# A second norm whose square, small operations and scaling stand one step later in the last chunk

## The chip, the cores and the metric

The kernel runs on the 8 cores of one Trainium2 chip, one batch element on each core, without any exchange between them. The metric is the device time of one execution in microseconds, taken for the slowest core.

## The reference

```python
x_dbl = einsum('bld,kd->blk', x, x_proj_w)           # 128 + 16 + 16 columns
delta = softplus(einsum('blr,dr->bld', x_dbl[..., :128], dt_proj_w) + dt_proj_b)
state = exp(delta * A) * state + delta * Bm * x      # a scan over 2048 tokens, 16 states
y     = einsum('bdn,bn->bd', state, c) + x * D_param
r     = layernorm(x + y)
e     = einsum('bln,nk->blk', r, weight) * scale     # 2048 x 2048
e     = e * tanh(|e|) / (|e| + eps), then clipped to a norm of 0.99
out   = layernorm(r + e)
```

x is (8, 2048, 2048), float32.

## The kernel before

The tokens of a core are taken in four chunks of 512 (chunk 0 to 3, LAST = 3). In a chunk there are 16 tiles of 128 channels, and for each of them 8 pairs of states: 128 steps to a chunk, 512 in all, numbered k. Step k of the scan is one instruction of VectorE (L1563). It takes decays from ScalarE (L1198 and L1200, two instructions for each step, issued two steps ahead) and inputs from TensorE (L881, into the two halves of pa). Five of eight steps then have their product with C made by GpSimd (g, L636) and summed by TensorE with an identity matrix (L841, L843); the other three are transposed by DMA from SyncE's queue (hT, L445) and multiplied on TensorE (L860). TensorE does this sum seven steps behind (LAG = 7), in the same in-order queue as the inputs of the next steps. After each tile of channels ScalarE evicts the sum as r_b (L1236), and the first sum of the next tile (L841) waits for that eviction by the semaphore r_ev.

Every engine's program is a loop over k, and all work beside the scans is put at written-out steps in it. While chunk c is scanned, the feed-forward part of chunk c - 1 runs beside it: transposes of r, a matrix product, a norm over the channels, and then for four blocks tb of 128 tokens the second layernorm. The blocks start at the steps S_R2 = (89, 98, 107, 116) of the chunk, and r2_at(k, after) says which block, if any, stands `after` steps behind its start at step k. A block goes as follows.

- after 0, ScalarE: scales eT by the factor ff and sums it (L1363).
- after 1, GpSimd: adds eT and rT into the buffer r2_b (L740, gpsimd_r2), and four small operations. In chunk 3 the add of blocks 1 to 3 first waits until the store of the block before has landed (out_p, L737).
- after 3, ScalarE: the square of r2_b with its sum (L1394, scalar_r2sq), which waits for the add.
- after 4, ScalarE: three small operations that make rq and nmr (L1374 to L1380).
- after 5: the norm itself, in place in r2_b. In chunks 1 and 2 ScalarE does it and SyncE stores it at after 6; in chunk 3 (blocks of chunk 2) GpSimd does it (L754, gpsimd_norm), waits for its own result and issues the store of 1 MB (L759).

There is one r2_b, so a block's add, square, norm and store exclude those of the next.

At the end of the last chunk SyncE transposes r (L490, the steps RT_LAST and then the rest); the first of these transposes waits until the add of block 3 is done (r2, L489), since that add reads the buffer rT that it overwrites. SyncE's queue is in order, and the transposes of h stand between those of r. After the last product and the last y matmul TensorE runs the rest of the feed-forward product for chunk 3 (tensor_rest, L1054), and then the norms of chunk 3 follow in series.

Of the kernel before, what the change touches and what calls it, by code (L numbers as in the profile page):

```python
# [21 lines left out]
STEPS = NDT * NP  # L22
# [30 lines left out]
LAST = NCH - 1  # L53
# [52 lines left out]
def n_row(c, name, tb=None):  # L106

    base = c * (len(ROWS) + NTB * len(PER_TB))
    if tb is None:
        return base + ROWS.index(name) + 1  # L110
    return base + len(ROWS) + tb * len(PER_TB) + PER_TB.index(name) + 1
# [11 lines left out]
def n_a2(c, tb):  # L123
    return c * NTB + tb + 1


def r2_at(k, after):

    for c in range(LAST):
        for tb in range(NTB):  # L130
            if (c + 1) * STEPS + S_R2[tb] + after == k:
                return c, tb
    return None
# [66 lines left out]
class K:  # L200
# [135 lines left out]
    def t(s, name):  # L336

        names = ("mean", "srr", "see", "r2sum", "r2sq", "lnq", "rq", "nmr",
# [4 lines left out]
        return s.tok[:, names.index(name), :]  # L343
# [183 lines left out]
    def gpsimd_program(s, e):  # L527
        S = s.sem
        for q in range(4):
            e.dma_start(out=s.c_xpw[:, q * 4:q * 4 + 4, :],  # L530
                        in_=s.xpw_d[:, q * 4:q * 4 + 4, :]
                        ).then_inc(S["xpw%d" % q], 16)
            s.gpsimd_x(e, 0, q)
        e.dma_start(out=s.c_dtw[:], in_=s.dtw_d).then_inc(S["dtw_in"], 16)
        s.tile_u(e, 0)
        for p in range(NH, 5):
            s.diag_b(e, 0, p, S["diag"])
        s.tile_u(e, 1)
        for p in range(5, NP):
            s.diag_b(e, 0, p, S["diag"])  # L540
        s.diag_c(e, 0, 0)
        for k in range(NK):
            c, st = divmod(k, STEPS)
            j, p = divmod(k, NP)
            if k > 0 and (k - 1) % NP in GP:
                s.gpsimd_cmul(e, k - 1)
            if k in (2, 4):
                s.diag_c(e, 0, k // 2)
            if p == 4 and j + 2 < NJ:
                s.tile_u(e, j + 2)  # L550
            if p == 6 and NDT <= j + 2 < NJ:
                s.gpsimd_carry(e, j + 2)
            for g in range(NKT):
                if k == S_CAST + SUM_GAP * g:
                    if g >= 2:
                        e.wait_ge(S["wc%d" % (g % 2)], g // 2 * 16)
                    e.dma_start(out=s.wbf_d[g], in_=s.wsw_d[g]
                                ).then_inc(S["wc%d" % (g % 2)], 16)
            for q in range(4):
                if c + 1 < NCH and st == (S_XQ if c > 0 else S_XQ0)[q]:  # L560
                    s.gpsimd_x(e, c + 1, q)
            if c + 1 < NCH and st >= STEPS - NP:
                s.diag_b(e, c + 1, st - (STEPS - NP), S["diag"])
            if 1 <= c < NCH and st + 1 in TP:
                s.diag_c(e, c, TP.index(st + 1))
            if 1 <= c <= LAST:
                s.token_values(e, c - 1, st)
            hit = r2_at(k, 1)
            if hit:
                s.gpsimd_r2(e, *hit)  # L570
            hit = r2_at(k, 5)
            if hit and hit[0] == LAST - 1:
                s.gpsimd_norm(e, hit[1])
        s.gpsimd_cmul(e, NK - 1)
        for kt in range(N_EARLY, NKT):
            s.load_w_rest(e, kt)
        for kt in range(NKT):
            s.gpsimd_prod(e, kt)
# [772 lines left out]
    def scalar_r2(s, e, k):  # L1351
        S = s.sem
        act = e.activation
        t = s.t

        def after_row(c, name, tb=None):
            e.wait_ge(S["row"], n_row(c, name, tb))

        hit = r2_at(k, 0)
        if hit:  # L1360
            c, tb = hit
            after_row(c, "ff")
            act(s.eT[:, tb, :], s.eT[:, tb, :], AF.Copy,  # L1363
                scale=t("ff")[:, tb:tb + 1],
                accum_out=t("r2sum")[:, tb:tb + 1]).then_inc(S["fe"], 1)
        if r2_at(k, 3):
            s.scalar_r2sq(e, *r2_at(k, 3))
        if r2_at(k, 4):
            c, tb = r2_at(k, 4)
            col = slice(tb, tb + 1)  # L1370
            n = n_a2(c, tb)
            after_row(c, "bq", tb)
            e.wait_ge(S["sq"], n)
            act(t("lnq")[:, col], t("r2sq")[:, col], AF.Ln, scale=RD,  # L1374
                bias=t("bq")[:, col]).then_inc(S["lnq"], 1)
            e.wait_ge(S["lnq"], n)
            act(t("rq")[:, col], t("lnq")[:, col], AF.Exp, scale=-0.5
                ).then_inc(S["rq"], 1)
            e.wait_ge(S["rq"], n)
            act(t("nmr")[:, col], t("nm")[:, col], AF.Copy,  # L1380
                scale=t("rq")[:, col]).then_inc(S["nmr"], 1)
        hit = r2_at(k, 5)
        if hit and hit[0] < LAST - 1:
            c, tb = hit
            col = slice(tb, tb + 1)
            e.wait_ge(S["nmr"], n_a2(c, tb))
            act(s.r2_b[:], s.r2_b[:], AF.Identity,
                scale=t("rq")[:, col], bias=t("nmr")[:, col]
                ).then_inc(S["o_ev"], 1)
# [220 lines left out]
```

## Time and profile before

| what | us |
|---|---|
| median of 3 runs | 1232.92 (1232.04 to 1249.09) |
| the profiled execution | 1232.44 |
| its span on the slowest core, core 4 | 1230.9 |
| VectorE busy in the span | 1152.6 |
| ScalarE busy | 996.6 |
| GpSimd busy | 961.0 |
| TensorE matmuls busy | 924.1 |

The profile is one execution. Times in its rows are microseconds from the start of the core's span. An idle time in brackets is that of the engine just before the instruction, with what the profile takes for its releaser; where an instruction waits for several semaphores, that is the one that came last by the profile. In rows that merge several instructions the duration covers all of them.

### The profile page before, as it was taken

What the parts mean: (1) busy time and instruction counts of PE and PEld (TensorE: products, weight loads), DVE (VectorE), ACT (ScalarE), POOL (GpSimd) and SP (SyncE); (2) the same over time, 40 slices, a digit from 0 to 9 for tenths busy, and PEclk for the clock granted to TensorE, in tenths of its full rate; (3) what the DMA queues carried; (4) which work ended last, traced back from release to release, by engine and by line L of the source; (5) the groups of instructions that cost most, each with busy time, mean ns of one, the idle gap of its engine ahead of it and who ended that gap; (6) DMA issues with size and microseconds to landing.
All of it is one profiled execution on the core that took longest, in us unless ns stands there. A gap on an engine that the chain in (4) does not pass through costs nothing.

```text
span 1230.9 us, 28298 instructions; the slowest of 8 cores (1222.2 to 1230.9 us)
## 1 busy us (share of the span) xinstructions
PE 924.1 (75%) x8772; PEld 587.1 (48%) x8932; DVE 1152.6 (94%) x597; ACT 996.6 (81%) x1730; POOL 961.0 (78%) x657
## 2 busy tenths in 40 slices
PE   4556666776689996666689997676569998688991
PEld 1344444544455554444455554444345555455551
DVE  1998999999999999999999999999999999998955
ACT  1676777777788899999877899999968798998854
POOL 2996766777997676898997677789998676789981
PEclk9597888888899999988789999888899999998995
DMA  8499979775659996245649997443468986357776
GB/s 114 102 134 142 137 117 148 118 123 99 138 91 186 159 181 102 54 99 106 141 84 168 183 161 121 66 96 108 122 111 141 179 151 132 55 141 166 183 162 168
DMA packets 337216, 159.67 MB, mean 130 GB/s; under 512 B 311280, under 2 KB 321104, under 8 KB 335280
## 3 DMA queue, kind: packets, MB, share of 16 engines
q1 hardware_dynamic: 326400, 134.66, 58.4%
q0 software_dynamic: 10672, 23.20, 11.5%
q8 instruction: 76, 1.25, 0.4%
q14 instruction: 68, 0.56, 0.2%
HBM read 83.29 MB, written 25.23 MB: 88 GB/s over the span
## 4 chain that ended last, share of the span: by engine, by line
ACT 26%; DVE 25%; issue 22%; PE 10%; POOL 9%; DMA 4%; SPq 1%; ACTq 1%; DVEq 0%; POOLq 0%; another core or an unknown queue 0%
DVE h L1563 25%; ACT dae_x L1200 12%; ACT dae_x L1198 7%; POOL g L636 4%; PE pa L881 2%; PE pb L961 2%; POOL r_b L740 2%; DMA c_dtw<-dtw 2%; DMA w_sl<-wbf 2%; ACT delta L1181 1%; PE pb L860 1%; ACT r_b L1236 1%; POOL diagC L659 1%; ACT delta L1187 1%; PE pa L1054 1%
## 5 line engine op out<-in xcount | busy, mean ns | idle before, releaser
L1563 DVE TENSOR_TENSOR_SCAN h<-dae_x,pa 128x1024 bf16<-128x1024 f32 x512 | 1118.2, 2262 | 23.8 <-PE pa L881 15.6
L636 POOL TENSOR_TENSOR g<-h,C_rep 128x1024 bf16<-128x1024 bf16 x320 | 678.4, 2127 | 194.0 <-DVE h L1563 185.0
L881 PE MATMUL pa<-diagB,uT 128*128 128x128 bf16 x4096 | 364.7, 232 | 224.0 <-DVE h L1563 212.4
L1198 ACT ACTIVATE dae_x<-delta,c_A 128x512 f32<-128x512 bf16 x512 | 367.0, 717 | 158.6 <-DVE h L1563 157.2
L881 PEld LDWEIGHTS pa<-diagB,uT 128*128 128x128 bf16 x4096 | 271.7, 102 | 397.0 <-issue 379.3
L1200 ACT ACTIVATE dae_x<-delta,c_A 128x511 f32<-128x511 bf16 x512 | 361.6, 706 | 0.0
L961 PE MATMUL pb<-r_b,w_sl 128*128 128x512 bf16 x747 | 192.5, 379 | 1.8 <-DMA w_sl<-wbf 0.7
L843 PE MATMUL pb<-g,eye_b 128*128 128x512 bf16 x319 | 132.7, 416 | 11.6 <-issue 3.7
L860 PE MATMUL pb<-diagC,hT 128*128 128x128 bf16 x1536 | 131.2, 235 | 0.5 <-DMA hT<-h 0.5
L860 PEld LDWEIGHTS pb<-diagC,hT 128*128 128x128 bf16 x1536 | 109.6, 107 | 21.4 <-issue 9.8
L961 PEld LDWEIGHTS pb<-r_b,w_sl 128*128 128x128 bf16 x768 | 71.9, 98 | 74.2 <-issue 2.2
L841 PE MATMUL pb<-g,eye_b 128*128 128x512 bf16 x213 | 89.0, 418 | 15.6 <-ACT r_b L1236 8.1
L612 POOL TENSOR_TENSOR u_b<-delta,x_b 128x512 bf16<-128x512 bf16 x64 | 75.0, 1171 | 21.8 <-ACT delta L1187 21.8
L889 PE MATMUL pa<-carry,eye_b 128*128 128x1 bf16 x768 | 75.0, 167 | 0.0
L889 PEld LDWEIGHTS pa<-carry,eye_b 128*128 128x128 bf16 x768 | 61.9, 102 | 0.2
L647 POOL TENSOR_TENSOR diagB<-eye_b,bcT 128x1024 bf16<-128x1024 bf16 x30 | 57.7, 1934 | 0.0
L740 POOL TENSOR_TENSOR r_b<-eT,rT 128x2048 f32<-128x2048 bf16 x12 | 48.8, 4069 | 9.6 <-ACT eT L1363 9.6
L992 PE MATMUL pb<-r_b,w_sl 128*128 128x512 bf16 x172 | 46.0, 387 | 1.9 <-DMA w_sl<-wbf 1.5
L841 PEld LDWEIGHTS pb<-g,eye_b 128*128 128x128 bf16 x320 | 33.9, 106 | 21.6 <-issue 21.5
L1181 ACT ACTIVATE delta<-pb,c_dtb 128x512 bf16<-128x512 f32 x64 | 42.9, 670 | 1.0 <-PE pb L815 0.9
L1236 ACT ACTIVATE r_b<-pb 128x512 bf16<-128x512 f32 x64 | 37.1, 579 | 7.3 <-PE pb L846 7.0
L1187 ACT ACTIVATE delta<-delta 128x512 bf16<-128x512 bf16 x64 | 39.4, 616 | 0.2
(187 smaller groups left out, 719.4 us busy)
## 6 DMA issues: line engine op xcount, KB each, us to landing
w_sl<-wbf SPq DMA_DIRECT2D x64, 512.0 KB, 4.5
wbf<-wsw POOLq DMA_DIRECT2D x16, 512.0 KB, 7.4
out<-r_b SPq DMA_DIRECT2D x8, 1024.0 KB, 4.3
x_b<-xT POOLq DMA_DIRECT2D x15, 512.0 KB, 8.5
C_rep<-bcscr SPq DMA_DIRECT2D x20, 256.0 KB, 4.5
out<-r_b POOLq DMA_DIRECT2D x4, 1024.0 KB, 5.6
hT<-h SPq DMA_TRANSPOSE x192, 3.8
out<-diagB SPq DMA_DIRECT2D x4, 512.0 KB, 6.2
```

Of the source, the lines that this page charges most:

```text
L612: e.tensor_tensor(s.u_b[:, j % 2, :], s.delta[:, j % 3, :], s.x_slot(j), ALU.mult).then_inc(S["u"], 1)
L636: e.tensor_tensor(s.g[:, g % NG, :, :], s.h[:, p, :, :], s.C_rep[:, GP.index(p), :, :], ALU.mult).then_inc(S["cmul"], 1)
L740: e.tensor_tensor(s.r2_b[:], s.eT[:, tb, :], s.rT[:, tb, :], ALU.add).then_inc(S["r2"], 1)
L841: e.matmul(s.ps_y, s.eye_b[:], s.g[:, g % NG, 0, :], start=(p == 0), stop=False)
L843: e.matmul(s.ps_y, s.eye_b[:], s.g[:, g % NG, 1, :], start=False, stop=False).then_inc(S["y_mm"], 1)
L860: mm = e.matmul(s.ps_y[:, tb * 128:(tb + 1) * 128], s.hT[:, w, n * NTB + tb, :], s.diagC[:, w, tb, n, :], start=False, stop=False, skip_gr ...
L881: mm = e.matmul(s.ps_b[:, k % 2, n, tb * 128:(tb + 1) * 128], s.uT[:, j % 3, tb, :], s.diagB[:, p, tb, n, :], start=True, stop=True, skip_ ...
L889: e.matmul(s.ps_b[:, k % 2, n, 0:1], s.eye_b[:], s.carry[:, j % 3, 2 * p + n:2 * p + n + 1], start=False, stop=True, skip_group_check=True)
L961: e.matmul(s.ps_f(g), s.w_sl[:, g % 2, i, :], s.r_b[:, ((c - 1) * NDT + i) % NR, :], start=(i == 0), stop=False)
L1198: e.activation(s.dae_x[:, k % 3, 0, :], s.delta[:, j % 3, :], AF.Exp, scale=s.c_A[:, n:n + 1])
L1200: e.activation(s.dae_x[:, k % 3, 1, 1:TL], s.delta[:, j % 3, 1:TL], AF.Exp, scale=s.c_A[:, n + 1:n + 2]).then_inc(S["dae"], 1)
L1563: e.tensor_tensor_scan(s.h[:, p, :, :].rearrange("p n t -> p (n t)"), s.dae_x[:, k % 3, :, :].rearrange("p n t -> p (n t)"), s.ps_b[:, k % ...
```

## The change

In the last chunk, which handles the four blocks of chunk 2, ScalarE's square goes from after 3 to after 4, its three small operations from after 4 to after 5, and GpSimd's norm with its store from after 5 to after 6. ScalarE's scaling (after 0) and GpSimd's add (after 1) stay, and so do the other chunks.

```diff
@@ gpsimd_program
             hit = r2_at(k, 1)
             if hit:
                 s.gpsimd_r2(e, *hit)
-            hit = r2_at(k, 5)
+            hit = r2_at(k, 6)
             if hit and hit[0] == LAST - 1:
                 s.gpsimd_norm(e, hit[1])
@@ scalar_r2
-        if r2_at(k, 3):
-            s.scalar_r2sq(e, *r2_at(k, 3))
-        if r2_at(k, 4):
-            c, tb = r2_at(k, 4)
+        late = k // STEPS == LAST
+        if r2_at(k, 3 + late):
+            s.scalar_r2sq(e, *r2_at(k, 3 + late))
+        if r2_at(k, 4 + late):
+            c, tb = r2_at(k, 4 + late)
```

## Rows read from the trace of the kernel before

**Rows 1.** The cores: span and mean granted clock.
```profile
core 0: 1228.6 us, clock 0.915
...
core 2: 1227.1 us, clock 0.919
...
core 4: 1230.9 us, clock 0.911
```

**Rows 2.** Busy time by stretch, core 4; the last row is of TensorE alone.
```profile
core 4: us, PE busy (x) PEld busy (x) DVE busy (x) ACT busy (x) POOL busy (x), PEclk, DMA share, GB/s
...
1088.00:1128.00 40.00, 31.85 (x274) 18.68 (x277) 34.77 (x16) 35.97 (x63) 37.70 (x28) 0.91 0.60 141
1128.00:1154.00 26.00, 25.44 (x243) 15.94 (x245) 25.76 (x13) 24.27 (x40) 24.59 (x18) 1.00 0.89 207
1154.00:1177.00 23.00, 20.33 (x184) 11.65 (x185) 20.54 (x10) 15.19 (x26) 21.69 (x14) 1.00 0.82 195
...
1121.40:1127.00 5.60, 5.35 (x27) 0.50 0.32 45
```

**Rows 3.** Timeline of VectorE, core 4: start, duration, instruction, idle time before.
```profile
1118.20 2.29 DVE L1563 TENSOR_TENSOR_SCAN h<-dae_x,pa 128x1024 bf16<-128x1024 f32 x1 [1.58 <-ACT dae_x L1200]
1120.87 2.29 DVE L1563 TENSOR_TENSOR_SCAN h<-dae_x,pa 128x1024 bf16<-128x1024 f32 x1 [0.38 <-ACT dae_x L1200]
1126.02 2.29 DVE L1563 TENSOR_TENSOR_SCAN h<-dae_x,pa 128x1024 bf16<-128x1024 f32 x1 [2.86 <-PE pa L881]
1128.55 35.00 DVE L1563 TENSOR_TENSOR_SCAN h<-dae_x,pa 128x1024 bf16<-128x1024 f32 x16 [0.24 <-PE pa L881]
```

**Rows 4.** Timeline of ScalarE, core 4.
```profile
1114.81 1.91 ACT L1394 ACTIVATE eT<-r_b 128x2048 bf16<-128x2048 f32 x1 [2.00 <-POOL r_b L740]
...
1120.60 0.57 ACT L1236 ACTIVATE r_b<-pb 128x512 bf16<-128x512 f32 x1
...
1157.86 1.91 ACT L1394 ACTIVATE eT<-r_b 128x2048 bf16<-128x2048 f32 x1 [1.16 <-POOL r_b L740]
```

**Rows 5.** Timeline of TensorE, core 4.
```profile
1121.43 0.58 PE L841 MATMUL pb<-g,eye_b 128*128 128x512 bf16 x1 [4.01 <-POOL g L636]
```

**Rows 6.** Timeline of GpSimd, core 4.
```profile
1088.09 4.08 POOL L740 TENSOR_TENSOR r_b<-eT,rT 128x2048 f32<-128x2048 bf16 x1 [1.85 <-ACT eT L1363]
...
1110.65 4.06 POOL L740 TENSOR_TENSOR r_b<-eT,rT 128x2048 f32<-128x2048 bf16 x1
...
1124.02 0.62 POOL L759 DMA_DIRECT2D out<-r_b  x1 [0.59 <-POOL r_b L754]
...
1132.47 4.07 POOL L740 TENSOR_TENSOR r_b<-eT,rT 128x2048 f32<-128x2048 bf16 x1 [0.39 <-ACT eT L1363]
...
1146.79 0.62 POOL L759 DMA_DIRECT2D out<-r_b  x1 [0.56 <-POOL r_b L754]
1147.44 6.31 POOL L636 TENSOR_TENSOR g<-h,C_rep 128x1024 bf16<-128x1024 bf16 x3
1153.71 4.05 POOL L740 TENSOR_TENSOR r_b<-eT,rT 128x2048 f32<-128x2048 bf16 x1
...
1172.95 4.30 POOL L636 TENSOR_TENSOR g<-h,C_rep 128x1024 bf16<-128x1024 bf16 x2 [0.23 <-DVE h L1563]
```

**Rows 7.** The four stores of L759, core 4, from issue to landing.
```profile
DMA to landing us min/median/max: 5.5/5.6/7.1
```

**Rows 8.** Timeline of SyncE's queue, core 4.
```profile
1157.85 3.81 SPq L490 DMA_TRANSPOSE rT<-r_b  x3
...
1172.62 1.23 SPq L445 DMA_TRANSPOSE hT<-h  x1
```

**Rows 9.** Timeline of TensorE at the end of the scans, core 4.
```profile
1176.10 0.61 PE L860 MATMUL pb<-diagC,hT 128*128 128x128 bf16 x8 [0.46 <-DMA hT<-h]
...
1177.39 0.38 PE L841 MATMUL pb<-g,eye_b 128*128 128x512 bf16 x1 [0.26 <-POOL g L636]
```

**Rows 10.** Chain that ended last, core 2.
```profile
1144.63 7.41 DMA out<-r_b
```

## Prediction

> **What bounds the kernel now.** I read the cores first. Core 4 is the slowest, 1230.9 us; cores 0 and 2 stand at 1228.6 and 1227.1 [rows 1]. The profiled execution took 1232.44 us, so 1.54 us lie around core 4's span, and the median of the runs, 1232.92, is 0.48 above it. All sums below are made on core 4 against 1232.44; the median is put in at the end.
>
> Then the busy times by stretch [rows 2]. The change acts between 1088 and 1177 us, where the four blocks of chunk 2 get their second norm beside the scans of chunk 3. VectorE is busy 34.77 of 40, 25.76 of 26 and 20.54 of 23 us; GpSimd 37.70 of 40, 24.59 of 26 and 21.69 of 23. Both are near full, so the question is which engine's waits can be given back.
>
> Third, VectorE's own row [rows 3]. It stops four times in the second block: 1.58 and 0.38 us for ScalarE's decay, 2.86 and 0.24 us for TensorE, 5.1 us in sum. ScalarE's row tells why [rows 4]: its square of block 1 (L1394) sat 2.00 us until GpSimd's add (L740) was done. The decays behind it came late (the first two stops), and so did the eviction r_b (L1236) at 1120.60 us. TensorE's L841 started at 1121.43 after 4.01 us of idling [rows 5]. The row names GpSimd's product, but this y matmul opens a new sum and needs the eviction too (r_ev, L840 and the line before), which ended at 1121.20; I charge the 4 us to it. After that stop TensorE had a granted clock of 0.50 for 5.6 us [rows 2], its lower level of 1.2 GHz, and VectorE's third stop contains that.
>
> Fourth, GpSimd's row [rows 6], of which VectorE's page says nothing. From the first add at 1088.1 to the last product at 1177.25 it waits only for its own norm before each store (0.59, 0.56 us), for ScalarE before the add of block 2 (0.39 us) and before the last two products (0.23 us). Everything else is work. Behind the last product TensorE's last y matmul starts at 1177.39 [rows 9], and the serial end of the kernel follows from there. So GpSimd, not VectorE, sets the end of the scans here, or something that GpSimd releases.
>
> Fifth, that something. On SyncE's queue the transposes of r start at 1157.85 [rows 8], when the add of block 3 (1153.71 plus 4.05) is done. Three of them, a transpose of h, two, another, two, and then the last transpose of h at 1172.62 run nearly without a gap; TensorE waited for it until 1176.10 [rows 9], 1.29 us ahead of the last product's matmul. On core 2 the chain runs wholly through here: store of block 2, 7.41 us, then the add of block 3, then these transposes [rows 10].
>
> **The change part by part.** Nothing is added or removed: four squares, twelve small operations, four norms and their four stores stand one step later.
>
> ScalarE, block 1. The square now stands behind one more decay pair (1.2 us of work) and the partial eviction. Both can run before 1114.7, when the add ends, since the scan two steps back is over. So the 2.00 us wait of [rows 4] disappears, the eviction comes some 2 us earlier and TensorE's 4.01 us wait mostly goes. VectorE gains between 2.0 us (only the stop before ScalarE) and the full 5.1 us of [rows 3]; I take 4.9, as all four stops hang on this one wait.
>
> GpSimd, order. The norm passes one product in blocks 0, 1 and 2 (2.1 us each, 6.31 for three [rows 6]); in block 3 no product stands between step 121 and 122, so only the wait for ScalarE moves. The amount of work is unchanged: 0 us by itself. The norm waits for ScalarE's small operations, but no such wait shows in GpSimd's row, and both move together: 0. Of the idle time the 0.39 and the 0.23 us can vanish, since ScalarE and VectorE are ahead: at best 0.62 us sooner.
>
> GpSimd, the stores. Each store is issued 2.1 us later, while the next add, which overwrites the same buffer r2_b, waits for it to land (out_p, L737). Landing takes 5.5 to 7.1 us here, 5.6 in the middle [rows 7]. Block 0 to 1: issued at about 1103.7, landed by 1109.4, and the add starts at 1110.65: covered [rows 6]. Block 1 to 2: issue at 1124.02 + 2.13 = 1126.15. With 5.6 us it lands at 1131.75, ahead of 1132.08, when GpSimd is free (1132.47 less 0.39): the add is 0.39 earlier. With 7.1, the longest of the four, it starts at 1133.35, 0.9 later than now. I take 0.4 later, between them. Block 2 to 3: issue at 1146.79 + 2.13 + 0.4 = 1149.3, and with its own 5.6 us and 0.13 us to the add the add starts at 1155.05 instead of 1153.71: 1.35 us later. Its bounds are 0.5 later (the earlier shift -0.39) and 3.9 later (7.4 us as on core 2 [rows 10], both times).
>
> The Trainium skill (DMA: Bandwidth & Descriptors, Anatomy of one DMA) gives a store from GpSimd's queue as about 2.0 us fixed plus bytes at 436 GB/s; for 1 MB that is an estimate of 4.4 us, and with it both stores would land before GpSimd is free and the change would cost nothing. The trace disagrees: 5.5 to 7.1 us, with 89% of the DMA engines' time taken around it [rows 7, 2]. I go by the trace.
>
> What it does to the end. GpSimd's stream ends 1.35 - 0.23 = 1.1 us later; SyncE's transposes start 1.35 us later, so the last transpose of h lets TensorE go at 1177.45 instead of 1176.10, still ahead of the last product's matmul at 1178.5. The later of the two decides: 1.1 us. VectorE's gain is spent on the way: ScalarE's squares of blocks 2 and 3 wait for adds that are not earlier, with VectorE some 5 us ahead, and then its decays are late. I expect stops of 2 us or more for VectorE near 1140 and 1160 us, and its last scan to end within 1.5 us of where it ends now. The start of this is there already: in block 3 ScalarE's square waited 1.16 us [rows 4].
>
> Other queues: the transposes of u and h on SyncE stand ahead of the add's wait and have 5 us more; the late weight loads that GpSimd issues after its last product move with it. For both I take 0 beside the 1.1 us.
>
> Sum: 1232.44 + 1.1 = 1233.5 on the profiled execution, 1234.0 against the median.
>
> **The rivals.** First, the store stays hidden: landing takes 5.5 us, TensorE and ScalarE are ahead and the last transfer meets less traffic. For it: 5.6 is the middle [rows 7]. Against: even then the add of block 3 waits, unless GpSimd is late itself. It gives -0.6 to +0.3 us, 1232.8.
>
> Second, faster: VectorE's 5.1 us [rows 3] are carried to the end. This is one mechanism: the wait of ScalarE at the square holds the decays, TensorE and VectorE, and if the products were only following the scans, all would end sooner. It decides as soon as GpSimd has idle time to give, and the products' row has 0.62 us of it. For it: VectorE is busy 1152.6 of 1230.9 us, more than any other engine. Against: [rows 6]. It gives 1232.92 - 5.1 = 1227.8.
>
> Third, slower by more: the stores land in 7.1 to 7.4 us both times (+3.9 us at most), and the idling of TensorE that moves from 1117 us to about 1160 us takes the granted clock to 0.50 there, where less slack is left. It gives about 1236.5.
>
> Fourth, the change does nothing: the store lands in time on core 4 and ScalarE's gain is lost; that is the first rival's number.
>
> **How the numbers follow.** Forecast, +0.4 to +2.5 us: 0.52. First rival and its like: 0.22. Second: 0.10. Third: 0.16. The range goes from 1230.9, which leaves out the second rival, to 1237.0, which leaves out the far end of the third. Two per cent, 24.7 us, is about what a measurement of this kernel can tell from no change; every case is inside: within 0.98, faster 0.01, slower 0.01.
>
> **What would show it.** Right: no wait of ScalarE at L1394 in block 1, TensorE's 4 us stop at 1117 gone and no half clock at 1121; an idle time of GpSimd before L740 in block 3 put down to the store, 0.5 to 3 us; new waits of ScalarE at L1394 in blocks 2 and 3 of over 2 us; SyncE's first transpose of r later by the same amount as the add. Wrong: last product over 1 us earlier than 1177.25, or no wait before the add.

## The result: slower by 0.41%, over four times the forecast

| | before | after |
|---|---|---|
| median | 1232.49 us | 1238.31 us |
| ratio, 95% interval | 1 | 1.0041 [1.0031, 1.0052] |
| profiled execution | 1232.44 us | 1240.42 us |
| slowest core in it | core 4, 1230.9 us | core 2, 1238.9 us |

The ratio is about 5.1 us of 1232.49; forecast were 1.1, and the median of after lies above the range's end of 1237.0. Some executions of both kernels are disturbed by a lower clock on one die; the ratio leaves them out. Each column of medians counts 14 runs.

The cores of after; they answer to [rows 1]:

```profile
core 0: 1222.6 us, clock 0.917
...
core 2: 1238.9 us, clock 0.919
core 3: 1238.7 us, clock 0.919
core 4: 1233.6 us, clock 0.910
```

Cores 2 and 3, which were at 1227.1 and 1222.2 us, are the slow ones now, at nearly unchanged clocks; core 4, on which all steps were worked out, is 2.7 us longer, and core 0 is shorter than it was. The program is the same on each core and the clocks are alike, so I looked for the difference in waits. To find it I cut each core's span at three instructions: the start of the first add (L740, block 0), the end of the last product (L636), and TensorE's last matmul. Between the first two GpSimd is full; I call them the full stretch and the serial end. Read from the timelines (before / after, us):

```
            first add at        full stretch     serial end      behind it
core 0      1088.6 / 1083.2     88.68 / 89.41    30.4 / 29.7     20.9 / 20.3
core 2      1086.3 / 1086.3     89.38 / 96.83    30.7 / 29.7     20.7 / 26.0
core 3      1082.8 / 1083.9     88.64 / 98.95    29.7 / 29.7     21.0 / 26.1
core 4      1088.1 / 1086.2     89.16 / 89.94    29.7 / 34.0     23.9 / 23.5
mean of 8   1085.5 / 1085.2     89.05 / 93.57    30.0 / 30.4     22.0 / 22.7
```

In the mean of the cores the full stretch has grown by 4.5 us and the serial end by 0.4: together 4.9. That is where the time went in this execution. It is a long one of the kernel after, and the ratio's 5.1 us are those of the slowest core: over all executions that the ratio counts, the mean of the eight cores' spans is 1230.8 us (standard error 0.4), against 1227.3 for the kernel before (72 such executions beside the experiments), which is 3.5 us more. (The first add differs by some us between cores and executions of either kernel. The last column is the landing of the last stores; it stood between 20.3 and 26.1 us in this execution, and cores 2 and 3 owe 5 us of their surplus in it to that. Its mean is 21.9 to 22.3 in the first eight experiments, whatever their change, so I take it for scatter of one execution.)

In after.py lines behind 1366 have moved by one: the scan is L1564, the square L1395. GpSimd's lines are the same. This is GpSimd's timeline on core 3 of after, against [rows 6]:

```profile
1099.52 0.65 POOL L759 DMA_DIRECT2D out<-r_b  x1 [0.61 <-POOL r_b L754]
1100.20 6.30 POOL L636 TENSOR_TENSOR g<-h,C_rep 128x1024 bf16<-128x1024 bf16 x3
1112.24 4.05 POOL L740 TENSOR_TENSOR r_b<-eT,rT 128x2048 f32<-128x2048 bf16 x1 [5.74 <-DMA out<-r_b]
...
1135.95 4.06 POOL L740 TENSOR_TENSOR r_b<-eT,rT 128x2048 f32<-128x2048 bf16 x1 [2.29 <-DMA out<-r_b]
...
1159.77 4.06 POOL L740 TENSOR_TENSOR r_b<-eT,rT 128x2048 f32<-128x2048 bf16 x1 [2.59 <-DMA out<-r_b]
```

The add of block 3 waits 2.59 us, within the 0.5 to 3 us foretold. The surprise is the first of these adds, that of block 1: 5.74 us behind the store of block 0, the one wait that was priced at nothing. The three make 10.6 us. The query of its landing says why; this is the store of block 0 alone, core 3 of after:

```profile
DMA to landing us min/median/max: 12.6/12.6/12.6
```

12.6 us, against 5.3 to 5.6 for block 0 on all eight cores before, and 5.5 to 7.1 for all four blocks in [rows 7]. On cores 0 to 7 of after block 0 landed in 6.3, 12.3, 10.6, 12.6, 7.4, 12.3, 8.7 and 11.1 us. Wherever it took over 7 us the add of block 1 waited (0.50 to 5.74 us). The stores of block 1 took 5.6 to 8.4 us, those of block 2 4.7 to 7.3 us, much as expected.

These waits are all of the growth. The three of a core make 1.0 to 10.6 us; taken off its full stretch they leave 88.3 to 88.4 us on every one of the eight cores. The kernel before has 88.6 to 89.2 us, with its one such wait (0.60 us, core 2) taken off.

The chain that ended last, core 3 of after (start, duration), against [rows 10]; all three stores are in it now:

```profile
1099.52 12.59 DMA out<-r_b
1112.24 4.05 POOL r_b L740
1127.68 8.13 DMA out<-r_b
1135.95 4.06 POOL r_b L740
...
1152.32 7.32 DMA out<-r_b
1159.77 4.06 POOL r_b L740
```

What ScalarE was to gain, on core 4 and core 3 of after, timeline of ScalarE, against [rows 4]:

```profile
1113.52 1.91 ACT L1395 ACTIVATE eT<-r_b 128x2048 bf16<-128x2048 f32 x1 [0.76 <-POOL r_b L740]
```

```profile
1116.38 1.91 ACT L1395 ACTIVATE eT<-r_b 128x2048 bf16<-128x2048 f32 x1 [5.97 <-POOL r_b L740]
```

The square of block 1 still waits: 0.76 us on core 4 instead of 2.00, but 5.97 us on core 3, where the add came late.

### The profile page after: what moved, and what is told of

It is laid out like the page before. It is cut to its first block, busy times and chain, and to the rows that moved or that the text cites. A ratio compares the mean times of both kernels' runs of the same rounds, so it can differ in the third digit from the quotient of the medians.

```text
span 1238.9 us, 28298 instructions; the slowest of 8 cores (1222.6 to 1238.9 us)
## 1 busy us (share of the span) xinstructions
PE 918.5 (74%) x8772; PEld 581.1 (47%) x8932; DVE 1152.9 (93%) x597; ACT 995.7 (80%) x1730; POOL 960.8 (78%) x657
## 4 chain that ended last, share of the span: by engine, by line
DVE 29%; ACT 26%; issue 22%; PE 9%; POOL 7%; DMA 5%; ACTq 1%; DVEq 0%; POOLq 0%; SPq 0%
DVE h L1564 29%; ACT dae_x L1200 12%; ACT dae_x L1198 7%; POOL g L636 3%; PE pa L881 2%; POOL r_b L740 2%; PE pb L961 2%; DMA c_dtw<-dtw 2%; DMA out<-r_b 1%; DMA uT<-u_b 1%; ACT delta L1181 1%; ACT r_b L1236 1%; PE pa L1054 1%; PE pb L860 1%; ACT delta L1187 1%
## 5 line engine op out<-in xcount | busy, mean ns | idle before, releaser
L1564 DVE TENSOR_TENSOR_SCAN h<-dae_x,pa 128x1024 bf16<-128x1024 f32 x512 | 1118.5, 2262 | 27.0 <-PE pa L881 12.4
L636 POOL TENSOR_TENSOR g<-h,C_rep 128x1024 bf16<-128x1024 bf16 x320 | 678.5, 2129 | 191.5 <-DVE h L1564 180.9
L881 PEld LDWEIGHTS pa<-diagB,uT 128*128 128x128 bf16 x4096 | 268.6, 102 | 411.9 <-issue 394.7
L843 PE MATMUL pb<-g,eye_b 128*128 128x512 bf16 x319 | 129.2, 405 | 10.6 <-DVE h L1564 3.5
L860 PE MATMUL pb<-diagC,hT 128*128 128x128 bf16 x1536 | 128.0, 231 | 1.6 <-DMA hT<-h 1.6
L860 PEld LDWEIGHTS pb<-diagC,hT 128*128 128x128 bf16 x1536 | 106.5, 104 | 19.5 <-issue 5.8
L841 PE MATMUL pb<-g,eye_b 128*128 128x512 bf16 x213 | 87.9, 413 | 14.9 <-ACT r_b L1236 11.0
L740 POOL TENSOR_TENSOR r_b<-eT,rT 128x2048 f32<-128x2048 bf16 x12 | 48.8, 4070 | 17.9 <-ACT eT L1363 9.5
```

What stands on the lines that cost most here:

```text
L636: e.tensor_tensor(s.g[:, g % NG, :, :], s.h[:, p, :, :], s.C_rep[:, GP.index(p), :, :], ALU.mult).then_inc(S["cmul"], 1)
L740: e.tensor_tensor(s.r2_b[:], s.eT[:, tb, :], s.rT[:, tb, :], ALU.add).then_inc(S["r2"], 1)
L841: e.matmul(s.ps_y, s.eye_b[:], s.g[:, g % NG, 0, :], start=(p == 0), stop=False)
L843: e.matmul(s.ps_y, s.eye_b[:], s.g[:, g % NG, 1, :], start=False, stop=False).then_inc(S["y_mm"], 1)
L860: mm = e.matmul(s.ps_y[:, tb * 128:(tb + 1) * 128], s.hT[:, w, n * NTB + tb, :], s.diagC[:, w, tb, n, :], start=False, stop=False, skip_gr ...
L881: mm = e.matmul(s.ps_b[:, k % 2, n, tb * 128:(tb + 1) * 128], s.uT[:, j % 3, tb, :], s.diagB[:, p, tb, n, :], start=True, stop=True, skip_ ...
```

## The experiments

Three theories stood at the start, with the letters that the texts written before each run use. S: the added waits of the adds for the stores, block 0's above all. A: something in ScalarE's part, whose gain is lost and may cost by itself. B: GpSimd's norm, one product later, holds the products back whether or not a buffer is free. The 88.3 to 88.4 us above already speak against B; the experiments ask all three. In the diffs only the deciding lines stand.

**One part alone.** The first kernel keeps the late ScalarE operations and takes GpSimd's norm and store back to after 5:

```diff
-            hit = r2_at(k, 6)
+            hit = r2_at(k, 5)
```

> ScalarE's square and small operations one step later, GpSimd's norm and store at the old step. Theory S (the loss is the add of the next block waiting for a store that is issued 2.1 us later and lands late): no wait of GpSimd before L740 beyond 0.6 us, ratio to the kernel before 0.997 to 1.001. Rival A (the later squares hold ScalarE and through its decays VectorE, 3 us at two blocks, and that is the loss): 1.003 or more, as the whole change.

The second is the kernel before with only `hit = r2_at(k, 6)` there, so GpSimd's part alone.

> Only GpSimd's norm and store one step later, ScalarE as in the kernel before. Theory S: waits before L740 in block 1 of 3 to 6 us on several cores, store of block 0 landing in 9 to 13 us on them, ratio 1.003 to 1.006. Rival A: ratio 0.999 to 1.001, since ScalarE is untouched.

```
                 full stretch, mean (range)   serial end   ratio to before
before           89.05 (88.6 to 89.4)         30.0         1
after            93.57 (89.4 to 99.0)         30.4         1.0041 [1.0031, 1.0052]
ScalarE alone    89.38 (88.5 to 90.2)         31.95        1.0026 [0.9999, 1.0053]
GpSimd alone     97.46 (94.2 to 102.0)        29.84        1.0086 [1.0066, 1.0106]
```

GpSimd's part alone costs twice what the whole change costs, more than the 1.003 to 1.006 expected, and all of it within the full stretch. ScalarE's part alone gives none of its 4.9 us. Its adds waited up to 0.99 us for a store, where 0.6 were expected at most, its ratio is above the expected range too, with an interval that just includes 1, and its serial end is 2 us longer. The two costs don't add up: on top of GpSimd's part, ScalarE's takes 3.9 us off the full stretch. The three waits for stores make 8.5 us in the mean of the cores with GpSimd's part alone and 5.2 us with the whole change; the stores of blocks 1 and 2 land in 8.1 and 7.3 us in the mean there, and in 6.6 and 5.8 us here. Of the 24 stores of blocks 0 to 2, 20 stand right behind a transpose with GpSimd's part alone and 8 with the whole change, in the sense of the table at the end of this section; that would explain it, and was not tested. GpSimd's timeline on the slowest core (core 6) of the second kernel:

```profile
1104.21 0.65 POOL L759 DMA_DIRECT2D out<-r_b  x1 [0.61 <-DVE h L1563]
1104.88 6.31 POOL L636 TENSOR_TENSOR g<-h,C_rep 128x1024 bf16<-128x1024 bf16 x3
1117.04 4.05 POOL L740 TENSOR_TENSOR r_b<-eT,rT 128x2048 f32<-128x2048 bf16 x1 [5.85 <-DMA out<-r_b]
...
1142.59 4.05 POOL L740 TENSOR_TENSOR r_b<-eT,rT 128x2048 f32<-128x2048 bf16 x1 [4.16 <-DMA out<-r_b]
...
1166.01 4.07 POOL L740 TENSOR_TENSOR r_b<-eT,rT 128x2048 f32<-128x2048 bf16 x1 [2.17 <-DMA out<-r_b]
```

The same wait stands before the add of block 1, so it doesn't need ScalarE's part. That speaks for S and against A as the main cause.

**Another place for the output.** The whole change, but the norm of blocks 0 to 2 writes to halves of eT and rT that are dead by then, in two instructions with two stores, and no add waits for a store.

```diff
+            for q, out in enumerate((s.eT[:, tb, :].bitcast(F32),
+                                     s.rT[:, tb, :].bitcast(F32))):
+                e.tensor_scalar(out, s.r2_b[:, q * half:(q + 1) * half],
...
-            e.wait_ge(S["out_p"], tb * 16)
```

> The whole change, but the norm of blocks 0 to 2 writes into dead parts of eT and rT in two halves with two stores, so that the next add waits for no store. Theory S: the waits of GpSimd before L740 are gone although the stores still land late; ratio 0.996 to 1.001. Rival A: still 1.003 or more. Rival B (the changed order on GpSimd, norm behind one more product, costs by itself): still 1.003 or more, with GpSimd busy all through.

The ratio was 1.0035 [1.0018, 1.0051], the full stretch 92.81 us. At a glance this speaks for B. The timeline of GpSimd, core 3, shows what it really is:

```profile
1096.92 0.65 POOL L763 DMA_DIRECT2D out<-eT  x1 [0.61 <-POOL eT L759]
...
1099.41 0.59 POOL L763 DMA_DIRECT2D out<-rT  x1 [0.59 <-POOL rT L759]
...
1106.30 4.06 POOL L740 TENSOR_TENSOR r_b<-eT,rT 128x2048 f32<-128x2048 bf16 x1
```

The wait before the add is gone. But the second store brings a second wait of GpSimd for its own result (0.59) and a second issue (0.59), and a second start of the norm: some 1.4 us a block on an engine that has none to give. All cores are alike here, 92.79 to 92.86, so the scatter of after is gone with the waits. The experiment put one cost in place of another and decides nothing on the sum. (Its stores of half the size landed in 3.4 to 7.0 us, not late as expected.)

**Block 0 put back.** The whole change, with only the norm and store of block 0 at its old step.

```diff
-            hit = r2_at(k, 6)
-            if hit and hit[0] == LAST - 1:
+            for after in (5, 6):
+                hit = r2_at(k, after)
+                if hit and hit[0] == LAST - 1 and (
+                        (hit[1] == 0) == (after == 5)):
```

> The whole change, but GpSimd's norm and store of block 0 stay at the old step. Theory S with the store of block 0 as the place: its store lands in 5 to 6 us, no wait in block 1, the waits in blocks 2 and 3 of up to 2.5 us remain; ratio 1.000 to 1.002, over half of the loss gone. Rivals A and B: over two thirds of the loss stay, 1.003 to 1.004.

The stretch went from 93.57 to 90.40 us (89.4 to 91.6), so the store of block 0 held 3.2 of its 4.5 us of growth, and 1.35 remain for blocks 1 and 2, about the size that the prediction gave them. The ratio, 1.0033 [1.0018, 1.0047], did not come down to what was expected. The serial end has part of the rest, 30.82 us against 30.0: both together are 2.2 us or 0.18%, the lower end of the interval. The mean of the eight cores over all executions that count is 1229.8 us (standard error 0.2), only 1.0 below the whole change and 2.5 above the kernel before. So the wait of block 1's add is gone on every core, but its share of the loss is 0.7 by this one execution's stretch and 0.3 by those means, and stays open between them. A second miss: the store of block 0 landed in 7.3 to 7.9 us on seven cores and in 5.2 us on one, where 5 to 6 were expected.

**A second buffer, nothing else added.** Two slots of eT that are dead by then hold blocks 1 and 3; the adds wait for no store but once, that of block 2 for the store of block 0. With late steps (the change) and with the steps of before:

```diff
+    def r2_of(s, c, tb):
+        if c == LAST - 1 and tb % 2 == 1:
+            return s.eT[:, tb - 1:tb + 1, :].rearrange(
+                "p b d -> p (b d)").bitcast(F32)
+        return s.r2_b[:]
...
-            e.wait_ge(S["out_p"], tb * 16)
+            if tb == 2:
+                e.wait_ge(S["out_p"], 16)
```

> The whole change, with the adds of blocks 1 and 3 in a second buffer (two dead slots of eT), so that no add waits for the store just issued; same instructions, same stores. Theory S (GpSimd is full from the first add to the last product, and what the change costs is the add's wait for a store): first add to last product 88.3 to 89.3 us on every core instead of 89.4 to 99.0 with the change; ratio 1.000 to 1.0025, what is left being TensorE's half clock in the serial end (last product to TensorE's end 31 to 32 us instead of 30). Rival B (the changed order on GpSimd): still 92 us or more and 1.004.

> The kernel before with the same second buffer. Theory S: its stores were hidden but for 0.6 us on one core, so first add to last product 88.6 to 89.1 us and ratio 0.999 to 1.001. If the stores cost more there than its trace shows, 0.997.

With the change: stretch 88.47 us (88.26 to 89.08), ratio 1.0019 [0.9999, 1.0040]. Without: 89.02 us, ratio 1.0002 [0.9993, 1.0011]. So the buffer by itself is worth nothing, and with it the change's stretch is even 0.6 us shorter than before. GpSimd on core 3 of the first of them, its L748 and L769 being the add and the store:

```profile
1101.79 0.65 POOL L769 DMA_DIRECT2D out<-r_b  x1 [0.61 <-POOL r_b L764]
...
1108.72 4.08 POOL L748 TENSOR_TENSOR eT<-eT,rT 128x2048 f32<-128x2048 bf16 x1
```

```profile
DMA to landing us min/median/max: 12.7/12.7/12.7
```

The second fence is the landing of that store: 12.7 us, as late as in after, and the add 6.9 us behind the issue waits for nothing. So the landing is late without the wait too, and lengthens this stretch only through it; with the 88.3 to 88.4 us above, that settles the stretch for S and against B. On the whole time the experiment says less. The middle of the loss falls from 0.41 to 0.19%, but the two intervals overlap from 1.0031 to 1.0040. In this execution nearly all of the loss is gone by the cores' means (-0.6 us in the stretch, +0.9 in the serial end, 30.91 us); over all executions that count the mean of the cores is 1228.7 us (standard error 0.6), 1.4 above the kernel before, where the change is 3.5 above. By both middle values the waits are at least half of the loss.

**The serial end.** ScalarE's part alone shows best what happens there. TensorE's timeline, core 2 of that kernel, against [rows 9]:

```profile
1169.96 0.38 PE L841 MATMUL pb<-g,eye_b 128*128 128x512 bf16 x1 [0.29 <-POOL g L636]
...
1174.08 1.01 PE L860 MATMUL pb<-diagC,hT 128*128 128x128 bf16 x8 [3.53 <-DMA hT<-h]
```

and the stretch behind it (columns as in [rows 2]):

```profile
1173.50:1180.30 6.80, 6.00 (x21) 2.78 (x23) 0.00 (x0) 0.60 (x1) 5.23 (x10) 0.52 0.99 213
```

TensorE waits 3.53 us for the last transpose of h (1.4 to 3.5 us on the eight cores), where before it was 0.46 us on core 4 and 1.84 at most; from 1173.50 the granted clock is 0.52 for 6.8 us, nearly all at its lower level of 1.2 GHz, and those matmuls are in series with everything behind them. All eight cores of this kernel have 3.1 to 6.1 us of such a clock within their serial end, which is 2 us longer than before. The scans end 4.5 us ahead of GpSimd's last product instead of 2.3, so VectorE did gain, and the gain turned into idling of TensorE at the worst place. Core 4 of after has the same:

```profile
1177.08 1.01 PE L860 MATMUL pb<-diagC,hT 128*128 128x128 bf16 x8 [4.29 <-DMA hT<-h]
```

Its full stretch was 89.94 us, 0.8 more than before, and its serial end 33.96.

What holds this transpose is its queue. Timeline of SyncE's queue on core 2 of ScalarE's part alone, against [rows 8]:

```profile
1165.02 4.17 SPq L490 DMA_TRANSPOSE rT<-r_b  x2
1169.34 1.25 SPq L445 DMA_TRANSPOSE hT<-h  x1
```

Two of the transposes of r stand just ahead of it, and none of these can start before the add of block 3 is done.

**The store off the full engine.** To see what GpSimd's place as the bound costs, the norm stays at its old step with the second buffer, and SyncE issues the stores at after 9; once with ScalarE late, once with the steps of before.

```diff
+            if r2_at(k, 9) and c == LAST:
+                tb = r2_at(k, 9)[1]
...
+                e.wait_ge(S["o_ev_p"], tb + 1)
+                e.dma_start(out=s.out_d[row:row + 128, :],
+                            in_=s.r2_of(LAST - 1, tb)
```

> ScalarE one step later, GpSimd's norm at the old step, second buffer, and the four stores issued from SyncE's queue (three steps behind the norm). It takes from GpSimd four waits for its own norm and four issues, 4 x (0.58 + 0.65) = 4.9 us. If GpSimd alone bounds this stretch: first add to last product 83.5 to 86 us, ratio 0.996 to 0.998. If VectorE, or SyncE's queue, is as near: 87 us or more and 0.999 to 1.001.

> The same stores from SyncE's queue and second buffer, but ScalarE's steps as in the kernel before. GpSimd is freed of the same 4.9 us, and so the add of block 1 may come sooner and ScalarE's wait of 2 us before its square with it. If the gain of e7_sp_store needs ScalarE's later step: first add to last product 87.5 to 89 us, ratio 0.999 to 1.001. If it does not: 84 to 86 us and 0.996 to 0.998, the same as e7_sp_store.

```
                          first add to last product   serial end   ratio to before
ScalarE late              83.40                       34.06        0.9986 [0.9974, 0.9999]
ScalarE as before         85.97 (85.1 to 86.5)        30.55        0.9987 [0.9977, 0.9997]
```

With GpSimd relieved, ScalarE's late steps bring 2.6 us of their 4.9 in the stretch. But 3.5 us more stand in the serial end, and the ratios are the same, neither as low as the 0.996 to 0.998 expected of a kernel that GpSimd alone bounds. TensorE and SyncE's queue, core 7 of the first (L873 is the former L860, L459 the former L445):

```profile
1167.74 0.61 PE L873 MATMUL pb<-diagC,hT 128*128 128x128 bf16 x8 [3.46 <-DMA hT<-h]
```

```profile
1160.28 0.52 SPq L403 DMA_DIRECT2D out<-eT  x1
1160.96 2.15 SPq L459 DMA_TRANSPOSE hT<-h  x1
```

**The transposes of r behind the last of h.** If that queue holds the end, moving three of the transposes of r behind the last one of h must give it back. The first kernel of the pair above and ScalarE's part alone, each with:

```diff
-RT_LAST = (120, 121, 121, 123, 123, 125, 125)
+RT_LAST = (120, 121, 121, 123)
```

> e7_sp_store with three transposes of r taken from ahead of the last transpose of h on SyncE's queue and issued behind it. In e7 the last product came 5.6 us sooner, but TensorE's serial end was 4 us longer: 3.5 us of waiting for that transpose of h, on most cores at the half clock afterwards. If the queue's order is the cause: wait gone, last product to TensorE's end 29.7 to 31 us instead of 34, ratio 0.994 to 0.997. If the landing of the transposes themselves is the limit: still 33 us or more and 0.998 to 0.999.

> e1_act_only with the same three transposes behind the last transpose of h. Its last product came as in the kernel before (89.4 us behind the first add), and TensorE's serial end took 32.0 us instead of 30.0 after a wait for the transpose of h and at the half clock. If that wait is the cause: 29.7 to 30.5 us, ratio 0.998 to 1.000. If the half clock comes from VectorE being done 4.5 us ahead of GpSimd whatever SyncE does: 31.5 us or more and 1.001 to 1.003.

The first: stretch 83.71, serial end 30.34 us, ratio 0.9972 [0.9958, 0.9985]. TensorE and SyncE's queue on core 7 now:

```profile
1165.51 0.61 PE L873 MATMUL pb<-diagC,hT 128*128 128x128 bf16 x8
```

```profile
1160.74 1.36 SPq L459 DMA_TRANSPOSE hT<-h  x1
1162.18 13.29 SPq L504 DMA_TRANSPOSE rT<-r_b  x9
```

The wait is gone, and 3.7 us of the serial end with it. The time moved less: the mean of the cores over all executions that count is 3.9 us below the kernel before beside it, where it was 1.8 below for the first kernel of the pair above. About 3.5 us or 0.28% are gained over before. (In this execution the stretch and the serial end give 5.0, and the last column takes 1.9 back, 23.9 us instead of 22.0; whether that belongs to the change is open.) Its interval lies below 1 and below that of after. So do those of the pair above; this one has the lowest middle. With ScalarE's part alone the serial end went from 31.95 to 30.64 us, and the ratio to 1.0018 [0.9995, 1.0042]; five of eight cores still had the half clock; on core 2 TensorE waited 0.67 and 1.47 us for GpSimd's last products instead. Those five cores have a serial end of 31.1 to 31.3 us, the other three of 29.7. So the queue's order holds a part of the 2 us, and another part comes, as the rival had it, with scans that end 4.5 us ahead of the last product. Its stretch is 90.16 us: on three cores the store of block 1 landed in 9.2 to 11.9 us, and the add of block 2 waited up to 3.98. Whether the 0.08% between it and ScalarE's part alone are real, these intervals don't say.

**What makes the store land late.** In after, SyncE's transpose of h begins just ahead of the store; before, the store goes ahead of it, 7.1 us behind the transpose before. SyncE's queue around it, core 3 of after (store at 1099.52) and core 4 of before (store at 1101.63):

```profile
1098.87 1.22 SPq L445 DMA_TRANSPOSE hT<-h  x1
...
1102.82 1.80 SPq L481 DMA_TRANSPOSE uT<-u_b  x1
```

```profile
1094.48 1.24 SPq L445 DMA_TRANSPOSE hT<-h  x1
...
1103.26 2.25 SPq L445 DMA_TRANSPOSE hT<-h  x1
```

On all cores of after the store of block 0 is issued 0.63 to 0.68 us behind that transpose. Two theories: it is the traffic of that stretch in general (then one product later it is no better), or this place right behind a transpose. The kernel before with the second buffer, and the issue of the store apart from the norm, one and two products later (r2_at(k, 7)); and the change with the second buffer, one product later (also 7):

```diff
+            hit = r2_at(k, 6)
+            if hit and hit[0] == LAST - 1:
+                s.gpsimd_store(e, hit[1])
```

> The kernel before with the second buffer, norms at the old step, and each store issued behind one more product (2.1 us later); no add waits for it. If the store of block 0 lands late because it meets the transpose of h and the weights of that moment: 8 to 13 us on at least half of the cores, as with the change. If its lateness belongs to the rest of the change (ScalarE's steps): 5.3 to 5.6 us as before.

> As e11_issue_one_later, but each store behind two more products (4.2 us later). If it is the meeting with one transpose and not a lasting load: back to 7 us or less for block 0 on most cores. If everything from here on is loaded: 8 us or more.

> e5_two_buf_after (the whole change with a second buffer) with each store issued behind one more product, 2 us later, so that the store of block 0 starts some 2 to 3 us behind the transpose of h instead of 0.65 us behind it. If the late landing comes from starting right behind a transpose: 5.5 to 7.5 us on all cores for block 0, where e5 and the change had 6.3 to 12.7. If the stretch itself is loaded with ScalarE and VectorE ahead: 8 us or more on half of the cores again.

Landing of block 0: 5.4 to 7.2 us in the first (8 to 13 had been expected of the traffic of the stretch, which falls by it), 6.0 to 7.2 in the second, 5.3 to 8.8 in the third, where it is issued 2.06 us behind the transpose (1.32 for the one with 8.8). In the first kernel the stores of block 1 took 12.5, 8.9, 11.9 and 11.7 us on cores 0, 3, 2 and 4, where they are issued 0.27 to 0.29 us behind a transpose, but 7.7 on core 6 in the same place. In the third those of block 1 stood 0.94 to 1.05 us behind one on six cores, and took 5.8 to 11.0.

All stores of blocks 0 to 2 of the eleven kernels in which GpSimd issues one store a block, by the time from the last start of a transpose on SyncE's queue to the store's issue:

```
issued behind a transpose by    stores   landed in over 8 us   longest
0.25 to 1.2 us                  76       37                    12.7
any other time                  188      7                     8.8
```

So a landing over 9 us happens only right behind a transpose, and even there in 28 of the 76 stores. Of the 37 landings over 8 us, 34 stand behind a transpose of h (61 stores) and 3 behind one of u (15 stores). The bounds 0.25 and 1.2 us were chosen on these same stores. The transposes aren't all of it either: with ScalarE late and the store of block 0 at its old step, 7.3 us behind a transpose, it landed in 7.3 us or more on 19 of 24 cores, where the kernel before has 5.3 to 5.6. The packets say a little more. In three kernels (after, its version with a second buffer, GpSimd's part alone) 22 stores of block 0 have this place, 0.42 to 0.68 us behind the same transpose of h. In 15 of them the first data packet moved within 2.1 us of the issue, beside the transpose, and they landed in 9.9 to 12.7 us. In the other 7, cores 0, 4 and 6 of after among them, it moved only after 2.9 us or more, and they landed in 6.3 to 9.4. In after the transpose went the same way: it landed in 9.1 to 12.1 us on the five cores whose store moved early, and in 5.3 to 8.0 on the other three. It looks as if store and transpose slow each other where their packets mix, and not where the store's come behind; that was read, not tested, and what decides which of the two happens stays open.

The times of single executions were 1240.49 us (first; on two of its cores the granted clock was 0.80 to 0.81 in the serial end, which took 34.6 and 36.0 us there), 1229.94 (second) and 1230.85 (third, against 1231.38 for the kernel before beside it). They say nothing of a ratio; the stretch was 86.39 us in the third and its serial end 32.56. Issued apart from the norm, three of its four stores have no wait of GpSimd for its own result before them, 0.56 to 0.61 us each with the issue right behind the norm; that is most of the 2.1 us below 88.47.

## Why the prediction was wrong

It had the sign and the mechanism, and four times too small a size. The step that failed is a term of the sum, "Block 0 to 1: issued at about 1103.7, landed by 1109.4, and the add starts at 1110.65: covered". Issue came as foretold: on core 4, 15.62 us behind the first add instead of 13.54. The landing of 5.6 us was taken over from a store that stood elsewhere among the transfers. Where it stands now it takes 6.3 to 12.6, and the term is 0.50 to 5.74 us on seven of eight cores and 3.4 us in the mean, not 0. It could have been asked: SyncE's queue of before, shown above, has a transpose at 1103.26 us, between the old place of the store (1101.63) and the new one (1103.7), and the prediction didn't look for it. It named "the transposes of u and h on SyncE" only to give them 0, and asked what the store does to them and not what they do to the store. The price could not be read from the trace of before: none of its stores of blocks 0 to 2 stands 0.25 to 1.2 us behind a transpose, and its longest landing, 7.4 us, would have given this term 0.6 us.

The other terms, by its order:

- GpSimd is full, and sets the end: right. What lengthened its stretch lengthened the kernel, and the three kernels that gained had 3.1 to 5.7 us taken off it.
- The norm passes one product in three blocks at no cost by itself: right. With the waits away the stretch is 88.47 us against 89.02.
- Block 1 to 2 "0.4 later": waits of 0.16 to 2.54 us on four cores, 0.09 on core 4. Block 2 to 3 "1.35 us later", bounds 0.5 to 3.9: waits of 0.30 to 2.59 us on seven, 0.96 on core 4. Together they leave 1.35 us in the mean, by the kernel with block 0 put back. Sized well.
- ScalarE's 2.00 us "disappears": only in part, 0.76 us on core 4. On core 3, where the add came late, it is three times as long. TensorE's stop on core 4, its timeline in after against [rows 5], is half:

```profile
1117.48 0.52 PE L841 MATMUL pb<-g,eye_b 128*128 128x512 bf16 x1 [1.90 <-ACT r_b L1236]
```

The releaser is now named as the eviction, to which the prediction had charged the 4.01 us. "No half clock at 1121" was wrong: core 4 has 3.4 us of it from 1117.60.

```profile
1117.60:1121.00 3.40, 3.40 (x17) 1.80 (x16) 1.60 (x1) 3.13 (x7) 3.40 (x4) 0.50 0.03 7
```

- "VectorE's gain is spent on the way", with stops of 2 us or more near 1140 and 1160: right in kind, on core 3 2.96 and 3.96 us, on core 4 only the second, 1.85 us. ScalarE's square of blocks 2 and 3 waited 3.25 and 5.09 us on core 3; on core 4 only that of block 3 did, 2.98 us. Timeline of VectorE, core 3 of after:

```profile
1143.50 19.86 DVE L1564 TENSOR_TENSOR_SCAN h<-dae_x,pa 128x1024 bf16<-128x1024 f32 x9 [2.96 <-ACT dae_x L1200]
...
1167.32 6.64 DVE L1564 TENSOR_TENSOR_SCAN h<-dae_x,pa 128x1024 bf16<-128x1024 f32 x3 [3.96 <-ACT dae_x L1200]
```

But the end was priced at the difference of the last waits, as if idling there cost only its own length. The lower clock behind it was given to the third rival alone, at 0.16. It came, on cores 1 and 4 (2.6 and 6.2 us of the serial end).

- The last transpose of h lets TensorE go 1.35 us later, "still ahead of the last product's matmul": wrong on core 4, and there this is the greater loss. SyncE's transposes did start later by as much as the add, 1.21 us, and the last one of h by 1.27. But it landed in 4.9 us instead of 3.3, TensorE took it 2.82 us later instead of 1.35 (counted from the first add) and behind the last product, after the 4.29 us of idling shown above, and the serial end grew from 29.7 to 34.0 us. On cores 2 and 3, the slowest, it stayed at 29.7.

Of the rivals, the first (store hidden) and the second (VectorE's 5.1 us carried) fall: ScalarE's part alone brought nothing. The third, landings of 7.1 to 7.4 us and half clock, came nearest with 1236.5; but the greater part lay in block 0 and not in blocks 1 and 2. The range was made from landings that stood in the trace, where the spread of one transfer in one place passed for the spread over all places.

On core 4, which the sums were made for, the full stretch grew by 0.8 us where 1.1 were forecast. That this core is 2.7 us longer, and not 1.1, is its serial end. But every core got its own landing, 6.3 to 12.6 us, and the kernel's time is that of the slowest core: a sum made on one core takes the best or the worst of eight draws for the rule.

The Trainium skill (DMA: Bandwidth & Descriptors, Anatomy of one DMA) gives an estimate of 4.4 us for this store by its sum of a fixed part and bytes; measured were 4.7 to 12.7 us. No sum of a fixed part and bytes can give both ends.

## What to carry to other kernels

Price a moved transfer by where it will start among the other queues' transfers, transposes above all, and not by the landing that it shows in its present place; where another engine waits for it, take the longest landing of its kind in the whole trace, on every core, and where no transfer of the trace stands in such a place, leave the range open upwards. Here even the longest would have been too short. An instruction on an engine that is full can be moved at no cost only if no wait comes with it; the second buffer was worth nothing by itself, but with it, giving the issue to another queue brought 0.14%, and 0.28% with the transposes of r behind the last of h, more than any order of the steps tried here. And a gain on an engine that isn't the bound arrives at the end of the stretch as idling of others, where it may cost a lower clock in the serial part.

## What was not expected of the hardware

In these kernels a 1 MB store from GpSimd's queue lands in 4.7 to 8.8 us, but in up to 12.7 us when it is issued 0.25 to 1.2 us behind the start of a DMA transpose on SyncE's queue. Both sides pay. The DMA issues of 1099 to 1113 us, core 3 of after, and those of 1101 to 1112 us, core 4 of before (size, median us to landing):

```profile
out<-r_b POOLq DMA_DIRECT2D x1, 1024.0 KB, 12.6
w_sl<-wbf SPq DMA_DIRECT2D x1, 384.0 KB, 6.0
w_sl<-wbf SPq DMA_DIRECT2D x1, 352.0 KB, 11.0
...
hT<-h SPq DMA_TRANSPOSE x3, 9.4
uT<-u_b SPq DMA_TRANSPOSE x1, 10.9
```

```profile
out<-r_b POOLq DMA_DIRECT2D x1, 1024.0 KB, 5.6
w_sl<-wbf SPq DMA_DIRECT2D x2, 352.0 KB, 5.1
...
hT<-h SPq DMA_TRANSPOSE x2, 4.7
uT<-u_b SPq DMA_TRANSPOSE x1, 4.6
```

The load of 352 KB and the transposes take twice as long as well (the one of 384 KB does not), and TensorE waited 5.67 us for such a load at 1113.45.

The second surprise is what TensorE's idling ahead of its last sum was followed by. With ScalarE's part alone it idled 1.4 to 3.5 us there for the last transpose of h, and on all eight cores 3.1 to 6.1 us at 1.2 GHz followed in the serial end, which was 2 us longer in the mean; on core 4 of after it was 4.29 us of idling and 6.2 us. It does not always follow: on core 7 of the kernel with ScalarE late and SyncE's stores the granted clock stayed at 1.00 for 14 us after 3.46 us of idling.
